# A graph network with an eigenvector layer on one core: the 512-deep stage of 21 pairs by seven products instead of eight, with sums on GpSimd

## The reference

```python
h = jnp.maximum(_layernorm(x, axis=-1), 0.0)
# layer 0; S = adj, so weighting = adj * adj; W1 256x512, W2 512x1024, W3 1024x256
h = relu(weighting @ (h @ W1)); h = relu(weighting @ (h @ W2))
x = x + weighting @ (h @ W3)
# layer 1; W1 256x128, W2 128x256
h = jnp.maximum(_layernorm(x, axis=-1), 0.0)
_, U = jnp.linalg.eigh(L_norm)            # of the normalized Laplacian of adj
x = x + U @ (relu((U.T @ h) @ W1 + b1) @ W2 + b2)
```

## Time and profile before

| what | value |
|---|---|
| median of 3 runs | 2438.76 us (2437.62 to 2440.72) |
| the profiled execution | 2439.07 us, its span 2437.3 us |
| TensorE busy | 2395.8 us, 11564 matmul instructions |
| VectorE busy | 1887.6 us |
| ScalarE busy | 877.5 us |
| GpSimd busy | 369.5 us |
| granted TensorE clock | 1.00 of full speed in all stages |
| end of the steps | about 1449 us (last addition of pair 20 starts at 1449.18) |
| start of pair 30 | about 2033 us |
| start of the second layer | about 2180 us |

### The profile page before, as it was taken

The page is one execution under the profiler, slowest core; times in us unless marked ns, Lnnn a source line. Parts: engine busy times, 40 slices in busy tenths (PEclk is TensorE's granted clock), DMA queues, the critical chain, the costliest instruction groups (busy, mean ns, idle before and its releaser), DMA issues.

```text
span 2437.3 us, 43265 instructions
## 1 busy us (share of the span) xinstructions
PE 2395.8 (98%) x11564; PEld 1987.3 (82%) x11564; DVE 1887.6 (77%) x10013; ACT 877.5 (36%) x2386; POOL 369.5 (15%) x1196
## 2 busy tenths in 40 slices
PE   6999999999999999999999999999999999999999
PEld 4778877777788877778788778888888888889998
DVE  6888888888887676666666779599999994337776
ACT  3333333333333333333433333233232232225554
POOL 1111101111111111111111131000101000013332
PEclk9999999999999999999999999999999999999999
DMA  2000000000000000000000000000000001004443
GB/s 98 26 27 27 17 18 18 27 26 26 27 26 9 27 26 18 27 26 26 27 26 27 27 26 27 24 12 27 19 24 26 26 26 61 18 21 131 133 133 108
DMA packets 90002, 89.76 MB, mean 37 GB/s; under 512 B 5376, under 2 KB 89088, under 8 KB 89856
## 3 DMA queue, kind: packets, MB, share of 16 engines
q1 hardware_dynamic: 89856, 88.23, 11.3%
HBM read 54.66 MB, written 33.55 MB: 36 GB/s over the span
## 4 chain that ended last, share of the span: by engine, by line
PE 95%; DVE 3%; ACT 1%; issue 0%; SPq 0%; DMA 0%; POOL 0%; DVEq 0%; ACTq 0%; POOLq 0%
PE ps L1136 79%; PE ps L1313 9%; PE ps L1087 4%; PE ps L1323 1%; PE ps L1260 1%; DVE A L659 1%; DVE col L712 1%; DVE xc L717 0%; DVE prods L703 0%; DVE A L663 0%; SPq L270 0%; DMA xl<-in_x_dram 0%; DVE col L700 0%; DVE xrow_sb L668 0%; ACT squares L448 0%
## 5 line engine op out<-in xcount | busy, mean ns | idle before, releaser
L1136 PE MATMUL ps<-agg2T,w 128*128 128x256 f32 x4096 | 925.4, 380 | 0.5
L1136 PEld LDWEIGHTS ps<-agg2T,w 128*128 128x128 f32 x4096 | 757.7, 190 | 106.1 <-ACT agg2T L487 5.3
L1136 PE MATMUL ps<-w,hid2T 128*128 128x256 f32 x2048 | 462.9, 379 | 0.0
L1136 PEld LDWEIGHTS ps<-w,hid2T 128*128 128x128 f32 x2048 | 380.6, 190 | 51.2
L448 ACT ACTIVATE squares<-xrow_sb 128x128 f32<-128x128 f32 (+9 forms) x254 | 81.7, 322 | 791.8 <-DVE xrow_sb L668 791.7
L1136 PE MATMUL ps<-w,aggT 128*128 128x512 f32 x512 | 234.6, 596 | 0.5
L1136 PE MATMUL ps<-weightT,hid 128*128 128x256 f32 x1024 | 232.6, 379 | 0.0
L350 POOL COPY Eb<-sc 128x1 f32 (+1 forms) x254 | 47.1, 185 | 1151.1 <-DVE v L687 1151.1
L487 ACT ACTIVATE hid2T<-ps 128x512 f32<-128x512 f32 x256 | 149.3, 585 | 199.1 <-PE ps L1136 199.1
L1136 PEld LDWEIGHTS ps<-weightT,hid 128*128 128x128 f32 x1024 | 189.7, 190 | 32.9 <-issue 8.2
L792 DVE RECIPROCAL pinv<-ahead 128x40 f32<-128x40 f32 (+1 forms) x768 | 215.4, 322 | 0.1
(11 more groups left out here) (305 smaller groups left out, 3481.5 us busy)
## 6 DMA issues: line engine op xcount, KB each, us to landing
xl<-in_x_dram SPq DMA_DIRECT2D x64, 256.0 KB, 2.8
xr<-in_x_dram SPq DMA_DIRECT2D x64, 256.0 KB, 2.8
x_dram<-xr SPq DMA_DIRECT2D x64, 256.0 KB, 2.3
xin<-x_dram SPq DMA_DIRECT2D x64, 256.0 KB, 2.8
out_dram<-xin SPq DMA_DIRECT2D x64, 256.0 KB, 2.2
w<-in_L_gnn_W_dram SPq DMA_DIRECT2D x1, 2048.0 KB, 10.2
w<-in_L_gnn_W_dram SPq DMA_DIRECT2D x1, 1024.0 KB, 11.1
w<-in_L_gnn_W_dram SPq DMA_DIRECT2D x1, 512.0 KB, 3.7
```

The source lines that it names most:

```text
L1136: ins = pe.matmul(dst, a, b, start=start, stop=stop)
```

## The change

In pairs 11 to 31 the stage `hid2` is computed for both graphs at once. Let B be the 512x512 matrix of the two graphs' `agg2` outputs side by side, and A one half (512x512) of W2 transposed. Each is cut into 2x2 blocks of 256x256, and A times B is made from seven block products (the Winograd form of Strassen's method) for each half of W2: 2 x 7 units `P1` to `P7` of 4 matmuls, 56 for 64. The operands that are sums of blocks and the outputs as sums of products are made by GpSimd:

- `sum_of_weights`: four sums per half of W2, eight in all, once, one behind each of the first eight steps of pair 10. They lie in `xin` slots 4 to 7, in `U`, `UT`, and in place of `adj_sb` and `adjT`.
- `sum_of_moving`: four sums per pair of `agg2` blocks.
- `add_products`: fourteen sums per pair (U2, C11, U4, U3, C22, C12, C21, for each half).

All are `tensor_tensor` over 128x512 with both inputs in SBUF. ScalarE copies each product out (14 evictions for 8) and applies relu in SBUF to each finished block (8 `finish` activations). `g3` waits for the finished blocks (semaphore `fin`) and is done in the order j = 1, 0, as are `res` and the additions to x. `placed` sets where in the 14 steps of a pair GpSimd's sums and ScalarE's evictions and finishes stand: the sums behind `keep_reflector`. Pairs 11 to 19 now have 14 steps each, so 20 pairs stand beside steps and 12 behind them. Loads of x1 into slots 4 to 7 wait for the last products. VectorE's instructions stay the same.

```diff
-                  (10, 11, 12, 0.54), (11, 14, 12, 0.54), (14, 17, 12, 0.54), (17, 19, 13, 0.54), (19, 21, 14, 0.54)]
+                  (10, 11, 12, 0.54), (11, 14, 14, 0.54), (14, 17, 14, 0.54), (17, 20, 14, 0.54)]
-        REFINE_AT, REFINE_EVERY, TURN_AT, VECTORS_AT = 14, 4, 56, 60
+        REFINE_AT, REFINE_EVERY, TURN_AT, VECTORS_AT = 14, 4, 54, 58
+        SEVEN_FROM = 11
+        PRODUCTS = [(p, half) for p in ("P1", "P6", "P2", "P5", "P7", "P3", "P4") for half in range(2)]
+        UNITS7 = [("agg", j, 0) for j in range(2)] + [("hid", j, q) for j in range(2) for q in range(NB)]
+        UNITS7 += [("agg2", j, q) for q in range(H1B // 2) for j in range(2)]
+        UNITS7 += [(p, half, 0) for p, half in PRODUCTS]
+        UNITS7 += [(st, j, 0) for st in ("g3", "res") for j in (1, 0)]
...
+        ADDS = [(name, half) for name in ("U2", "C11", "U4", "U3", "C22", "C12", "C21") for half in range(2)]
...
+        def placed(steps, share):
+            filled = beside(steps, share, WORK7)
+            tau = 65.0 / steps
...
+            for name, half in ADDS:
+                start = max(free, evicted[AT7[LAST_OF[name], half, 0]])
+                free = start + 1.45
+                summed.append(int(max(start - 3.2, 0) // tau))
...
+            where = turned + summed
+            where = [min(where[n:]) for n in range(len(where))]
+            for n, s in enumerate(where):
+                pool_turns[s].append(("T", n + 1) if n < 4 else ("add", n - 4))
...
-            for b in range(SLOTS2):
+            for b in range(SLOTS2 // 2):
                 load_one(b, b)
             save_pair(PAIRS - 2)
             load(xres, load_xr, PAIRS - 1)
+            sp.wait_ge(unit, done7(PAIRS - 1) + AT7["g3", 1, 0])
+            for b in range(SLOTS2 // 2, SLOTS2):
+                load_one(b, b)
...
+            def sum_of_moving(pair, n):
+
+                a, b = {1: (agg2T[:, 1, 0:2, :], agg2T[:, 0, 0:2, :]), 2: (agg2T[:, 1, 2:4, :], moving_sum(1)),
+                        3: (agg2T[:, 1, 2:4, :], agg2T[:, 1, 0:2, :]), 4: (agg2T[:, 0, 2:4, :], moving_sum(2))}[n]
+                pool.wait_ge(evac, done7(pair) + AT7["agg2", 1, 0 if n == 1 else 1] + 3)
+                if n in (2, 4):
+                    pool.wait_ge(turn_s, 4 * pair - 4 * SEVEN_FROM + n - 1)
+                pool.tensor_tensor(moving_sum(n), a, b, ALU.subtract).then_inc(turn_s, 1)
+
+            def add_products(pair, n):
...
+                pool.wait_ge(evac, done7(pair) + AT7[LAST_OF[name], half, 0] + 3)
+                if after:
+                    pool.wait_ge(added, len(ADDS) * pair - len(ADDS) * SEVEN_FROM + ADD_AT[after, half] + 1)
+                pool.tensor_tensor(dst, a, b, ALU.add).then_inc(added, 1)
...
                         keep_reflector(steps * t + (k0 - steps * first) + s, blocks(k0)[0])
+                        if last == SEVEN_FROM and s < len(S_TURNS):
+                            if s == 0:
+                                pool.wait_ge(load_w, 16 * 7)
+                            sum_of_weights(*S_TURNS[s])
...
+                        for kind, n in pool_turns[s]:
+                            if kind == "T":
+                                sum_of_moving(t, n)
+                            else:
+                                add_products(t, n)
...
             with pool.Fori(WITH_STEPS, PAIRS - 1) as t:
-                for j in range(2):
-                    ln_minus_mean(t + 1, j)
-                    ln_scale(t + 1, j)
-                for j in range(2):
-                    add_x(t, j)
+                strassen_sums(t, True)
+                for j in (1, 0):
+                    add_x(t, j, True)
+            strassen_sums(PAIRS - 1, False)
...
+            def finish(pair, n):
+
+                act.wait_ge(added, len(ADDS) * pair - len(ADDS) * SEVEN_FROM + ADD_AT[FINS[n]] + 1)
+                block_ = hid2_block(*FINS[n]).rearrange("p a n -> p (a n)")
+                act.activation(block_, block_, ACT.Relu).then_inc(fin, 1)
...
+            LN_AFTER = {0: [(0, 0)], 3: [(1, 0)], 4: [(0, 1)], 5: [(2, 0)], 7: [(1, 1)], 9: [(2, 1)]}
+            FINS_AFTER = {9: [0, 1], 11: [2], 12: [3], 13: [4, 5, 6, 7]}
...
+                if stage[0] == "P":
+                    b11, b12, b21, b22 = (agg2T[:, c, 2 * k:2 * k + 2, :] for k in range(2) for c in range(2))
+                    left, right = {"P1": (w2_block(j, 0, 0), b11), "P2": (w2_block(j, 0, 1), b21),
+                                   "P3": (weight_sum(j, 4), b22), "P4": (w2_block(j, 1, 1), moving_sum(4)),
+                                   "P5": (weight_sum(j, 1), moving_sum(1)), "P6": (weight_sum(j, 2), moving_sum(2)),
+                                   "P7": (weight_sum(j, 3), moving_sum(3))}[stage]
+                    return sum([group(half[c], [(left[:, d, P * c:P * c + P], right[:, d, :]) for d in range(2)])
+                                for c in range(2)], [])
...
+                if stage == "g3" and first in (0, 4):
+                    block_ = (("C11", "C21"), ("C22", "C12"))[j][first // 4]
+                    pe.wait_ge(fin, len(FINS) * pair - len(FINS) * SEVEN_FROM + FIN_AT[block_, 1] + 1)
```

More of the change, by code:

```diff
@@ L382, in _ @@
             for (first, last, steps, share), k0 in zip(GROUPS, FIRST_STEP):
+                pool_turns = placed(steps, share)[2] if seven(first) else [[]] * steps
                 with pool.Fori(first, last) as t:
@@ L494, in _ @@
             for (first, last, steps, share), k0 in zip(GROUPS, FIRST_STEP):
-                work_beside = beside(steps, share)
+                if seven(first):
+                    early_events, late_events, _ = placed(steps, share)
+                    with act.Fori(first, last) as t:
+                        for s in range(steps):
+                            step_root(steps * t + (k0 - steps * first) + s, columns(k0))
+                            for kind, n in early_events[s]:
+                                event(t, kind, n)
+                            for j, at in enumerate(LN_AT):
+                                if 0 <= s - at < 6 and (s - at) % 2 == 0:
+                                    LN[(s - at) // 2](t + 1, j)
+                            for kind, n in late_events[s]:
+                                event(t, kind, n)
+                    continue
+                work_beside = beside(steps, share, WORK)
                 with act.Fori(first, last) as t:
@@ L550, in pair_body @@
                         continue
-                    evacuate(pair, i)
-                    for j in range(2):
-                        if more and AT["hid2", j, 0] <= i < AT["hid2", j, 0] + len(LN):
-                            LN[i - AT["hid2", j, 0]](pair + 1, j)
-                    if not more and i == AT["hid2", 1, 2]:
+                    evacuate7(pair, i)
+                    for part_of_ln, j in LN_AFTER.get(i - FIRST_P, []) if more else []:
+                        LN[part_of_ln](pair + 1, j)
+                    for n in FINS_AFTER.get(i - FIRST_P, []):
+                        finish(pair, n)
+                    if not more and i == AT7["P4", 1, 0]:
                         normalise(0, 0)
@@ L1156, in _ @@
                 bl = blocks(k0)
-                work_beside = beside(steps, share)
+                work_beside = beside(steps, share, WORK7 if seven(first) else WORK)
+                part_of = work7 if seven(first) else work
                 with pe.Fori(first, last) as t:
@@ L1187, in _ @@
             with pe.Fori(WITH_STEPS, FIRST_ROUND) as t:
-                for f in range(len(FRAGS)):
+                for f in range(len(FRAGS7)):
                     fragment(t, f)
@@ L1307, in _ @@
                     part(arg)
[L1308 removed]
+                fragment(PAIRS - 2 + n // len(FRAGS7), n % len(FRAGS7))
             def run(mms):
```

183 lines of the change are left out of this document (158 added, 25 removed).

## The result

| | before | after |
|---|---|---|
| median | 2438.24 us (4 runs) | 2654.71 us (4 runs, 2653.41 to 2662.2) |
| the profiled execution | 2439.07, span 2437.3 | 2655.73, span 2654.0 |
| end of the steps | 1449.2, with 21 pairs | 1532.6, with 20 pairs |
| start of the second layer | 2180.0 | 2396.8 |

The ratio is 1.0892, 95% interval [1.0878, 1.0906]: slower by 9%. The forecast was slower by 5%, 2568 us; the range, 2460 to 2670, held the time, near its upper end: the change costs 216 us where I had said 129.

What follows compares the result with a forecast made beforehand. TensorE, busy 98% of the span, was taken to bound the kernel. Steps' end 1493.4 + counts 121 + searches 555 + last pairs 140.4 + second layer 257.3 = 2567.1 us span; forecast 2568, range 2460 to 2670.

Steps and rivals of the forecast that it cites:

- the full lock: Rival: sums cost VectorE 1.1 us each, or finishes hold the steps' roots too; total 2694 us, chance 0.10.
- to the turning of the counts: From the steps' end: TensorE needs 120.1 us, VectorE's counts 121 with some 28 sums; 121 taken.
- searches, until the norm: Second search stretch: 144 more sums add 108 us to VectorE, giving 555 us; TensorE stands 63 us at pair 30.
- the last two pairs: Pairs 30 and 31, beside the refinement: 140.4 us, including 4 us for a late sign stage.
- Fewer matmuls: Eight fewer per pair at 0.431 us save 3.45 us; a bare pair falls to 58.67, 21 pairs save 72.4.
- A step beside a pair: Pairs with 14 steps: TensorE 62.9 us, VectorE 65.1 to 58.7; 64 us a pair before GpSimd's sums.
- the first rival: The sums cost nothing, because they find VectorE waiting in the steps of pairs 11 to 19: 2370 us, chance 0.09.
- The price of a sum: Each 128x512 GpSimd sum delays VectorE 0.75 us on average, 13.5 us a pair; pairs beside steps take 77.5.
- held in the searches only: Rival: the steps find room for the sums (64.5 us a pair), the searches don't: 2449 us, chance 0.06.
- One that reads PSUM is not: Shared SBUF access: GpSimd's sums hold VectorE instructions with two SBUF inputs, not one that reads PSUM.
- held in the steps only: Rival: sums delay the steps but not the searches, whose chains alternate with reciprocals not held: 2505 us, chance 0.12.
- The cover of the rest: Costed at nothing: loads of slots 4 to 7, and ScalarE's extra evictions and finishes (0 to 2 us a pair in the range).

Runs made afterwards that it cites:

- narrow_all: Changed kernel with all 18 GpSimd sums per pair cut from 128x512 to 128x2, every wait and place kept: 2407.55 us, ratio 0.9867.
- repack: Kernel before with only the change's grouping of steps (14 steps in each of pairs 11 to 19): 2448.43 us, ratio 1.0037.
- before_sums: Kernel before plus 18 useless 128x512 GpSimd additions per pair in pairs 11 to 20, nobody waiting for them: 2556.62 us, ratio 1.0481.
- narrow_steps: Changed kernel with the sums cut to 128x2 only in pairs 11 to 19, those beside steps: 2512.35 us, ratio 1.0297.
- last_two_late: Kernel before with seven products only in pairs 30 and 31, second turning and vectors four fragments later than in the change: 2431.45 us, ratio 0.9971.
- narrow_after: Changed kernel with the sums cut to 128x2 only in pairs 20 to 31, those behind the steps: 2553.70 us, ratio 1.0466.
- last_two: Kernel before with seven products only in pairs 30 and 31, second turning and vectors placed as in the change: 2440.64 us, ratio 1.0007.
- fill: Changed kernel plus three useless 256-column matmuls behind six steps of each of pairs 11 to 19: 2650.31 us, ratio 1.0865.

## Why the prediction was right, and where its sizes were off

The mechanism and both places were as forecast; the size was not. The change costs 216 us, of which the forecast had 129, and 2654.7 lies nearer to the rival *the full lock* (2694) than to 2568. The range held because it reached up to near that rival. By the steps of the prediction, in spans:

| step | forecast | measured | off by |
|---|---|---|---|
| pair 10 with the weight sums, its end | 795.9 | 793.6 | -2.3 |
| pairs 11 to 19 | 697.5 | 739.0 | +41.5 |
| to the turning of the counts | 121 | 138.4 | +17.4 |
| searches, until the norm | 555 | 576.6 | +21.6 |
| the last two pairs | 140.4 | 149.2 | +8.8 |
| second layer | 257.3 | 257.2 | -0.1 |

The norm is ready at 2247.6, from where the last two rows count. Together +86.9 us: 2567.1 became 2654.0. The rival's pair beside steps, 83.8 us, is close to the 82.1 measured, but by another sum: its 1.1 a sum on a base of 64, where the runs show 0.88 on 66.3.

Of the signs that I had named, the 336 instructions, the bare pair of 58.7 (58.9 to 59.1), the waits of TensorE for the column and the stop at pair 30 came. The pairs beside steps are longer than the 74 to 81 us that I gave. Lines 708 and 712 are longer, but 717 is not (24.3 us before, 21.1 now in the 126 steps) and 671 hardly (44.4 and 47.5); lines 700 and 684 are, which I had not named.

**Fewer matmuls: right to 7%.** In the changed kernel the second x additions of two bare pairs, two pairs apart, start 118.19 us apart (timeline of GpSimd; before's are in the earlier trace rows):

```profile
1814.05 1.26 POOL L487 TENSOR_TENSOR xr<-xr,res 128x512 f32<-128x512 f32 x1 [0.38 <-ACT res L663]
...
1932.24 1.26 POOL L487 TENSOR_TENSOR xr<-xr,res 128x512 f32<-128x512 f32 x1 [0.33 <-ACT res L663]
```

That is 59.1 a pair; pairs 24 to 29 of narrow_all take 58.9 each, where before took 62.1. Eight matmuls of the stage were worth 3.2 us, 0.40 each, for my 0.431.

**A step beside a pair: the base was 66.3 us, not 64.** I had taken the larger of two averages over 14 steps, TensorE's 62.9 and VectorE's 58.7 to 65.1, and added little for the filling. Narrow_all has no wide sums, only the two x additions of a pair, and takes 66.29: TensorE busy for 574.97/9 = 63.9 (1.0 over my 62.9) and idle for 2.4, VectorE idle for 16.7. So a pair is longer than the larger average: over nine pairs, 9 x (66.28 - 64) = 20.5 us. Over half of it is TensorE's wait for the finishes, once in each of the nine pairs (waits of narrow_all in this stage; line 676 is `finish`, 1384 the pairs' matmuls):

```profile
PE ps L1384 <- ACT hid2T L676: 11.8, 9, 1.4
PE ps L1298 <- DVE xc L928: 8.8, 12, 2.2
```

These 1.3 us a pair are in the changed kernel too, 11.8 us in all, and neither before nor repack has such a wait. I had put the finishes at nothing in the sum, with 0 to 2 us a pair kept for the range. The roots of the steps were not held up by them: VectorE waits 50.5 us for the roots in narrow_all, 50.1 in repack. Of the 8.8 us for the column one part can be followed: pair 13 takes 69.8, its neighbours 66.7 and 65.7, and there the two x additions of pair 12 hold lines 700 and 712 one after the other and the clock falls to 0.5 for 3.4 us. The idle 20 us a pair, which I had named as an argument for the first rival, took 0.13 of 0.78 us in before_sums.

**The price of a sum: 0.88 us beside steps, not 0.75.** (82.11 - 66.28)/18 from the changed kernel's mean pair and that of narrow_steps. VectorE's instructions, each laid beside the same one of before, are 136.5 us longer in these pairs, 0.84 a sum. My 0.75 was a mean of two kinds: the additions of before come in twos once a pair, and the first of two adds 1.03 us to VectorE in the mean, the second some 0.5. The change's come up to three in a row (the timeline above), and there too the first adds most: 0.91 in the mean, the second 0.83, the third 0.80. In before_sums, with the same rows of three, a sum costs VectorE 0.78. So the length of a row does not explain the price; where in VectorE's round a sum falls does matter, as the two half additions show. Nine pairs: 9 x 18 x 0.13 = 21 us. The price lay between the bounds of 0.33 and 1.1. It is below the sum's own 1.27, since VectorE isn't always asking. (The prediction's estimate of about 2740 for 1.27 on every sum is some 2754 by its own terms, and *held in the searches only* has 3 us in its 1373.4 that stand nowhere.)

**"One that reads PSUM is not" held: wrong for line 700.** Its scalar is from PSUM, but its two tensors, vn and A, are both in SBUF. It is line 905 above, 1.16 for 0.22, and over pairs 11 to 19 the line with the largest growth, 33.8 us; then 708 (30.7), 684 (29.1) and 712 (20.0). For these lines the two tensor inputs count, and line 703 (908), with one of them in PSUM, was indeed free. The next paragraph has a second kind.

**Pair 10: 2.9 us, not 6.** 72.1 us for 69.2. The eight sums are one to a step there, and each met VectorE, always in line 696 (901 now). One of them, GpSimd and then VectorE:

```profile
724.70 1.29 POOL L496 TENSOR_TENSOR xin<-w 128x512 f32<-128x512 f32 x1
```

```profile
724.75 1.27 DVE L901 TENSOR_SCALAR qn<-qcol,sc 128x2 f32<-128x2 f32 x1
```

VectorE's instructions in the pair are 7.9 us longer, and 5.0 of it went into idle time. Line 696 has a single tensor input, two elements wide. In the whole changed kernel 13 such instructions of 128x2 begin beside an addition, and all 13 are held, by 0.93 to 1.11 us; of 90 of 128x1 none is, nor any of 142 reciprocals. So "both tensor inputs in SBUF" is not the whole rule: a TENSOR_SCALAR with one input of two elements was held as well.

**The counts: 36 sums, not 28, and 0.99 each.** All the sums of both pairs came before the counts were done. VectorE's instructions in the stretch are 35.6 us longer, and TensorE stood for 12.8 us, where I had both just in time.

**The searches: the wait was right, with 0.91 for 0.75 a sum.** 144 sums made VectorE 131.3 us longer, against 108. The Sturm update (line 795, now 1000) went from 221 to 393 ns in the mean; the reciprocals between kept their length, 370 and 368. That they alternate did not spare the updates, as the rival *held in the steps only* would have had it. TensorE stood for 75.5 us before pair 30's evictions; I had said 63.

**The last two pairs.** Pair 31 took 76.6 us against 68.3 with the turning at its later place and wide sums (last_two_late), and against 68.3 with narrow ones (narrow_after). The changed kernel shows the wait of last_two again, 5.1 us before line 1515, and its 305 instructions take 71.21 us for 68.05 at a mean clock of 0.96. Pair 30 starts, after the stop, at the lower clock, and its 319 instructions take 74.82 us where they take 71.70 in last_two_late (timeline of TensorE):

```profile
2248.37 9.99 PE L1378 MATMUL ps<-w,aggT 128*128 128x512 f32 x16 [75.48 <-ACT aggT L663]
```

I had given the sign stage 4 us and the clock nothing; the wait of 5.1 us and the two losses by the clock, 3.1 and 3.2, are most of the 12.8 us over the bare work of 136.4 (139.8 less the two units done while it stands).

**The cover of the rest held in part.** The loads of slots 4 to 7 cost nothing that shows: the second layer is 0.1 us shorter. The finishes cost 1.3 us a pair beside steps, as above.

## What to carry to other kernels

Moving work to an idle GpSimd isn't free for VectorE: count how many of VectorE's instructions on the deciding chain have both tensor inputs in SBUF, and price every GpSimd instruction that reads two SBUF inputs at the greater part of its own length (0.78 to 0.99 of 1.27 us here), unless it can be released exactly when VectorE waits. How much of such a delay an engine's idle time takes can't be read from the idle time: it took a sixth with 18 whole additions a pair and two thirds with one half addition a step. Test it by adding idle work to the kernel before, which needs no rewriting. A chain of new waits behind the fewer matmuls has a price of its own (here TensorE's wait for the finishes, 1.3 us a pair of the 3.2 saved). And a saving per matmul pays only in the stretches where TensorE is the last to arrive: here two pairs of 21 made a kernel faster than both.

## What the runs showed of the hardware beyond this

- Beside a GpSimd addition of 128x512, VectorE's TENSOR_SCALAR of 128x2 in SBUF was held 13 times of 13 (0.93 to 1.11 us), that of 128x1 0 times of 90.
- A GpSimd instruction that only writes SBUF (128x1150, 1.06 us, 162 times) changed VectorE's time in the steps by 0.04 us in all; one that reads two inputs (1.27 us) cost it 0.84 each.
- TensorE's clock: in the 50 us in which TensorE stood (2190 to 2240) the granted clock is 0.50, the lower level of 1.2 GHz. In the steps it fell to that level 12 times, for 3.4 to 6.8 us. The stage's mean was 0.97; with useless matmuls in it 0.99, and the stage was 1.6 us shorter (fill). In pair 31, where TensorE bounds, one such fall after a wait of 5 us cost 2.6 to 3.2 us more, and after the stop of 75.5 us the lower clock cost 3.1 us.
- One 128x256 addition per step cost the kernel 0.27% behind `keep_reflector` and 0.03% ahead of it, with the same instruction and the same count: where in a step of some 5.2 us a GpSimd instruction begins decides.
